# Attention of a two-layer kernel: heads taken in pairs, value matmuls of four heads together, all transposes in transpose mode

## What is computed

```python
qkv = einsum('bnc,fc->bnf', layernorm(x), w_qkv)     # 12 heads of 16 channels, 4 images, 256 tokens
att = softmax(q @ k.T * SCALE)                        # 256 x 256 per head and image
att = softmax(att * mask)                             # mask is 0.5 where row % 64 == column % 64, else 1
out = (att @ v) @ w_out.T + b_out
```

## Time and profile before

| | us |
|---|---|
| median of 3 runs | 545.7 |
| lowest and highest run | 543.4, 549.63 |
| span of the profiled execution, first to last instruction | 538.7 |
| TensorE busy in the span | 477.6 |
| VectorE busy | 235.1 |
| ScalarE busy | 162.4 |
| GpSimd busy | 152.3 |

### The profile page before, as it was taken

One profiled execution on the slowest core, in us unless ns is written; L12 is line 12 of the kernel. 1 busy time (PEld: TensorE's weight loads), 2 busy tenths in 40 slices (PEclk: granted clock), 3 DMA queues, 4 the chain that ended last, 5 costly groups with the idle time before them and its releaser, 6 DMA issues.

```text
span 538.7 us, 7851 instructions
## 1 busy us (share of the span) xinstructions
PE 477.6 (89%) x2343; PEld 322.5 (60%) x2344; DVE 235.1 (44%) x676; ACT 162.4 (30%) x418; POOL 152.3 (28%) x135
## 2 busy tenths in 40 slices
PE   0999999999998169899999999889999999999990
PEld 0554766565656147766676666655767666666660
DVE  5157232222222344676666665638623333333330
ACT  2142002111112023466656565442012111121210
POOL 2000115556655100000000000000125565566652
PEclk9999699999999669899999999999899999999996
DMA  9992111222220593000000003764211221221100
GB/s 265 209 350 67 35 52 23 39 38 35 39 27 9 141 331 135 1 1 0 2 1 1 1 2 83 181 174 112 77 38 31 33 25 26 34 35 23 12 0 0
DMA packets 20956, 36.20 MB, mean 67 GB/s; under 512 B 6544, under 2 KB 17481, under 8 KB 20484
## 3 DMA queue, kind: packets, MB, share of 16 engines
q1 hardware_dynamic: 10468, 29.56, 19.3%
q0 software_dynamic: 10464, 6.33, 8.4%
HBM read 31.92 MB, written 8.45 MB: 75 GB/s over the span
## 4 chain that ended last, share of the span: by engine, by line
PE 69%; DMA 15%; DVE 6%; issue 5%; ACT 1%; POOL 1%; POOLq 1%; SPq 0%; DVEq 0%
PE bank L1158 15%; DMA sum<-y,slot_tok 12%; PE bank L1333 9%; PE bank L1097 8%; PE bank L1173 6%; PE bank L1320 6%; PE bank L1127 4%; PE bank L1275 4%; PE bank L1289 3%; PE bank L1165 2%; PE bank L1322 2%; PE bank L1368 2%; PE bank L1134 1%; PE bank L1079 1%; PE bank L1304 1%
## 5 line engine op out<-in xcount | busy, mean ns | idle before, releaser
L473 POOL DMA_INDIRECT rows<-xn_rows,slot_tok x56 | 58.4, 1042 | 131.5 <-DVEq L800 90.6
L1158 PE MATMUL bank<-w_first,rows_t 96*128 x248 | 85.4, 487 | 0.2 <-issue 0.2
L1173 PE MATMUL bank<-w_second,hid_t 128*128 x370 | 71.4, 333 | 8.3 <-issue 6.3
L859 DVE TENSOR_SCALAR y<-bank,slot_w 128x192 f32<-128x192 f32 x54 | 22.6, 418 | 102.5 <-PE bank L1173 83.6
L1173 PEld LDWEIGHTS bank<-w_second,hid_t 128*128 128x128 f32 x370 | 58.7, 190 | 13.5 <-issue 13.1
L484 POOL DMA_INDIRECT out<-y,slot_tok x31 | 48.9, 1577 | 47.4 <-DMA out<-y,slot_tok 28.2
L1158 PEld LDWEIGHTS bank<-w_first,rows_t 96*128 96x128 f32 x248 | 44.6, 190 | 25.5 <-issue 0.7
L631 ACT ACTIVATE scratch<-bank,neg_max 128x256 f32<-128x256 f32 x96 | 44.6, 470 | 39.2 <-DVE neg_max L948 34.4
L1333 PE MATMUL bank<-scratch,w_first 128*32 128x256 f32 x192 | 50.9, 390 | 0.0
L522 POOL COPY act_h<-o_inv 128x256 f32<-128x256 f32 x12 | 4.8, 400 | 162.7 <-DVE o_inv L979 162.0
L484 POOL DMA_INDIRECT sum<-y,slot_tok x23 | 36.3, 1577 | 36.3 <-DMA sum<-y,slot_tok 23.7
(11 more groups left out here) (172 smaller groups left out, 649.3 us busy)
## 6 DMA issues: line engine op xcount, KB each, us to landing
w_first<-in_gate_up SPq DMA_DIRECT2D x16, 576.0 KB
w_second<-in_down SPq DMA_DIRECT2D x1, 4608.0 KB, 24.5
w_first<-in_fc SPq DMA_DIRECT2D x1, 3072.0 KB
w_second<-in_fc SPq DMA_DIRECT2D x1, 3072.0 KB, 28.5
xn_rows<-xn_tok SPq DMA_DIRECT2D x2, 768.0 KB, 5.9
rows<-xn_rows,slot_tok POOLq DMA_INDIRECT x56, 2.7
w_first<-in_x_t SPq DMA_DIRECT2D x2, 384.0 KB, 4.4
w_first<-in_w SPq DMA_DIRECT2D x1, 768.0 KB, 7.0
```

The source lines that it names most:

```text
L473: pool.indirect_dma_start(rows[b % 2][:], None, xn_rows[L.l], bass.IndirectOffsetOnAxis(slot_tok[:, b:b + 1].bitcast(U32), 0), bounds_chec ...
L1158: ins = pe.matmul(bank[:, 5 + g, 0:I1], rows_t[0:CH, k, :], w(CH, (k * 2 + g) * I1, I1), start=(k == 0), stop=(k == NCH - 1))
L1173: ins = pe.matmul(bank[:, 1, 0:C], hid_t[:, tile(ic)], w(P, ic * C, C), start=(ic == 0), stop=(ic == L.IC - 1))
```

## The change

Two heads now make one unit of work p (24 of them) in every step of the attention: one reduction over two banks, four exponentials, one reciprocal and four products (in place in `e1`), eight transposes to banks 4 and 5, one exponential over 1024 elements. All transposes are in transpose mode. The value matmuls of a chunk stand together once its second pair is ready, ordered by key tile and within it by head, so that neighbours write to different column groups. The sums stand in bank 6 beside the values and the spread inverses in bank 7. The buffers are regrouped: `p2_t` takes the room of `xn_t` and `g_sh` for two of its three. The steps of each engine are written in a new order. In the diff, lines that are only "..." mark what is left out.

```diff
-        e1 = [scratch_at(512 * i, 2, TOKENS_IMG) for i in range(3)]
-        att = [scratch_at(512 * (3 + i), 2, TOKENS_IMG) for i in range(2)]
-        p2_t = [scratch_at(512 * (5 + i), 2, TOKENS_IMG) for i in range(3)]
+        e1 = [scratch_at(1024 * i, 4, TOKENS_IMG) for i in range(3)]
+        p2_t = [scratch_at(3072, 4, TOKENS_IMG),
+                xn_t_room[:, 0, :].rearrange("p (a b) -> p a b", a=4),
+                g_room[:].rearrange("p a (b c) -> p (a b) c", b=2)]
...
         N_HEADS = IMAGES * HEADS
...
+        N_PAIRS = N_HEADS // 2
+        N_CHUNKS = N_HEADS // HPC
+        PAIRS_CHUNK = HPC // 2
+        def chunk_at(p, lag):
+            c = (p - lag + 1) // PAIRS_CHUNK - 1
+            if c == N_CHUNKS - 1 or (p - lag + 1) % PAIRS_CHUNK or c < 0 or c >= N_CHUNKS:
+                return None
+            return c
+        SUMS_AT = TOKENS_IMG
...
-            sp.wait_ge(sc_ps, N_HEADS)
+            sp.wait_ge(sc_ps, N_PAIRS)
...
...
+            def exp_scores(p):
+                act.wait_ge(nmax_ready, p + 1)
+                if p >= 3:
+                    act.wait_ge(att_t_ps, p - 2)
+                for q in range(4):
+                    ins = nc.scalar.activation(e1[p % 3][:, q, :], bank[:, 2 * (p % 2) + q // 2, (q % 2) * 256:(q % 2 + 1) * 256],
+                                               ACT.Exp, bias=neg_max[:, p % 4, q:q + 1],
+                                               accum_out=exp_sum[:, p % 4, q:q + 1])
+                ins.then_inc(e1_ready, 1)
+            def exp_att(p):
+                act.wait_ge(att_t_ps, p + 1)
+                if p >= 3:
+                    act.wait_ge(av_ps, (p - 3) // PAIRS_CHUNK + 1)
+                nc.scalar.activation(p2_t[p % 3].rearrange("p a b -> p (a b)"),
+                                     bank[:, 4:6, :].rearrange("p a b -> p (a b)"), ACT.Exp).then_inc(p2_ready, 1)
...
-            for n in range(N_HEADS + 3):
-                if n < N_HEADS:
-                    exp_scores(n)
-                if 0 <= n - 2 < N_HEADS:
-                    exp_att(n - 2)
-                if chunk_at(n, 3) is not None:
-                    out_copy(chunk_at(n, 3))
+            exp_scores(0)
+            exp_scores(1)
+            for p in range(N_PAIRS):
+                if p + 2 < N_PAIRS:
+                    exp_scores(p + 2)
+                exp_att(p)
+                if chunk_at(p, 1) is not None:
+                    out_copy(chunk_at(p, 1))
+            out_copy(N_CHUNKS - 1)
...
-            def neg_maximum(n):
-                dve.wait_ge(sc_ps, n + 1)
-                v.tensor_reduce(neg_max[:, n % 4, :], bank[:, n % 4, :].rearrange("p (a b) -> p a b", a=2),
+            def neg_maximum(p):
+                dve.wait_ge(sc_ps, p + 1)
+                b = 2 * (p % 2)
+                v.tensor_reduce(neg_max[:, p % 4, :], bank[:, b:b + 2, :].rearrange("p b (a k) -> p (b a) k", a=2),
                                 AXX, ALU.max, negate=True).then_inc(nmax_ready, 1)
...
-            def attention(n):
-                dve.wait_ge(e1_ready, 2 * n + 2)
-                if n >= 2:
-                    dve.wait_ge(att_t_ps, n - 1)
-                go(v.reciprocal(exp_inv[:, n % 2, :], exp_sum[:, n % 4, :]))
-                for qt in range(2):
-                    ins = v.scalar_tensor_tensor(att[n % 2][:, qt, :], e1[n % 3][:, qt, :], exp_inv[:, n % 2, qt:qt + 1],
+            def attention(p):
+                dve.wait_ge(e1_ready, p + 1)
+                go(v.reciprocal(exp_inv[:, p % 2, :], exp_sum[:, p % 4, :]))
+                for q in range(4):
+                    ins = v.scalar_tensor_tensor(e1[p % 3][:, q, :], e1[p % 3][:, q, :], exp_inv[:, p % 2, q:q + 1],
                                                  mask, ALU.mult, ALU.mult)
-                    if qt == 0:
+                    if q < 3:
                         step(ins)
                 ins.then_inc(att_ready, 1)
...
-            for n in range(ATT_STEPS):
-                if 2 <= n < N_HEADS:
-                    neg_maximum(n)
-                if 0 <= n - 1 < N_HEADS:
-                    attention(n - 1)
-                if n == N_HEADS:
-                    ln_stats(0)
-                if chunk_at(n, SUMS) is not None:
-                    invert_sums(chunk_at(n, SUMS))
-                if n == ATT_STEPS - 1:
-                    ln_rows(2, 0)
-                if chunk_at(n, SUMS + 2) is not None:
-                    out_norm(chunk_at(n, SUMS + 2))
-                if (chunk_at(n, SUMS + 3) or 0) % HC == HC - 1:
-                    residual(chunk_at(n, SUMS + 3) // HC)
+            for p in range(N_PAIRS):
+                if p + 2 < N_PAIRS:
+                    neg_maximum(p + 2)
+                attention(p)
+                if chunk_at(p, 2) is not None:
+                    invert_sums(chunk_at(p, 2))
+                if chunk_at(p, 3) is not None:
+                    out_norm(chunk_at(p, 3))
+                if (chunk_at(p, 4) or 0) % HC == HC - 1:
+                    residual(chunk_at(p, 4) // HC)
+            ln_stats(0)
+            out_norm(N_CHUNKS - 2)
+            invert_sums(N_CHUNKS - 1)
+            ln_rows(2, 0)
+            out_norm(N_CHUNKS - 1)
+            residual(IMAGES - 1)
...
-            def scores(n):
-                pair, img = (n, n + 1), n // HEADS
-                if n >= 4:
-                    pe.wait_ge(e1_ready, 2 * (n - 2))
+            def scores(p):
+                pair, img = (2 * p, 2 * p + 1), 2 * p // HEADS
+                if p >= 2:
+                    pe.wait_ge(e1_ready, p - 1)
                 for qt in range(2):
                     q0 = img * TOKENS_IMG + qt * P
                     for part in (k_high, k_low):
...
                             ins = pe.matmul(bank[:, m % 4, qt * 256:(qt + 1) * 256], q_parts[r, h // HPC, q0:q0 + P],
                                             part[r, h // HPC, img * TOKENS_IMG:(img + 1) * TOKENS_IMG],
                                             start=(part is k_high), stop=(part is k_low))
-                            if qt == 1 and part is k_low:
-                                ins.then_inc(sc_ps, 1)
+                ins.then_inc(sc_ps, 1)
             pe.wait_ge(parts_ready, 2 * QKC)
             scores(0)
+            scores(1)
...
-            def att_transpose(n):
-                pe.wait_ge(att_ready, n + 1)
-                if n >= 2:
-                    pe.wait_ge(p2_ready, n - 1)
+            def att_transpose(p):
+                pe.wait_ge(att_ready, p + 1)
+                if p:
+                    pe.wait_ge(p2_ready, p)
+                for m in range(2):
+                    for kt in range(2):
+                        for qt in range(2):
+                            ins = pe.transpose(bank[:, 4 + m, (kt * 2 + qt) * P:(kt * 2 + qt + 1) * P],
+                                               e1[p % 3][:, 2 * m + qt, tile(kt)], ident)
+                ins.then_inc(att_t_ps, 1)
+            def weigh_values(c):
+                pe.wait_ge(p2_ready, PAIRS_CHUNK * (c + 1))
+                if c:
+                    pe.wait_ge(o_raw_ready, c)
+                    pe.wait_ge(inv_ready, c)
+                img = c // HC
                 for kt in range(2):
-                    for qt in range(2):
-                        dst = bank[:, 4 + n % 2, (kt * 2 + qt) * P:(kt * 2 + qt + 1) * P]
-                        src = att[n % 2][:, qt, tile(kt)]
-                        if kt == qt:
-                            ins = pe.matmul(dst, src, ident, start=True, stop=True)
-                        else:
-                            ins = pe.transpose(dst, src, ident)
-                ins.then_inc(att_t_ps, 1)
-            def weigh_values(n):
-                img, h = n // HEADS, n % HEADS
-                g, c = n % HPC, n // HPC
-                pe.wait_ge(p2_ready, n + 1)
-                if g == 0 and c:
-                    pe.wait_ge(o_raw_ready, c)
-                for kt in range(2):
-                    ins = pe.matmul(bank[g * HG:(g + 1) * HG, 6, 0:TOKENS_IMG],
-                                    v_tok[:, 2 * img + kt, h, :], p2_t[n % 3][:, kt, :],
-                                    start=(kt == 0), stop=(kt == 1))
+                    for g in range(HPC):
+                        p = c * PAIRS_CHUNK + g // 2
+                        ins = pe.matmul(bank[g * HG:(g + 1) * HG, 6, 0:TOKENS_IMG],
+                                        v_tok[:, 2 * img + kt, (c % HC) * HPC + g, :], p2_t[p % 3][:, 2 * (g % 2) + kt, :],
+                                        start=(kt == 0), stop=(kt == 1))
                 ins.then_inc(av_ps, 1)
...
-            for n in range(ATT_STEPS):
-                if n % 2 and n + 1 < N_HEADS:
-                    scores(n + 1)
-                if 0 <= n - 2 < N_HEADS:
-                    att_transpose(n - 2)
-                if 0 <= n - 3 < N_HEADS:
-                    weigh_values(n - 3)
-                if chunk_at(n, SUMS) is not None:
```

(67 more changed lines are left out.)

22 lines of the change are left out of this document (5 added, 17 removed).

## The result

| | before | after |
|---|---|---|
| median of 4 runs, us | 547.66 | 611.61 |
| lowest, highest | 543.4, 552.43 | 608.3, 617.42 |
| span of the profiled execution | 538.7 | 612.1 |

The ratio is 1.1215, 95% interval 1.1119 to 1.131: 64 us slower. The changed kernel's profiled execution took 614.11, 2.0 us more than its span, and all executions in this study whose span is known took 1.8 to 2.2 us more. So the kernel before's profiled execution took near 541 and was faster than the median, and the 7.0 us that the prediction laid around the span were 5 too many. Executions of one kernel can lie 2% and more apart, the longer ones with a lower mean clock, and a profile shows one execution only, which in the kernels lag, lag_act, lag_act_oldT, lag_act_fill, before_values and before_values_newT was one of the longer ones.

The account below looks back on a forecast made before the run. It took TensorE, 89% busy, as the bound. Span 538.7 + 38 for the new order + 38 for the low clock = 615, with 7.0 around the span about 621, given as 620; range 581 to 652.

Parts of the forecast that it names:

- the ring: Attention in the new order: TensorE and VectorE each wait while the other works, 4.92 us a step.
- values fully overlapped: Rival for the value matmuls: four column groups at once, 1.0 us a chunk for 2.1; result 603, chance 0.17.
- Part 1: Attention transposes: 96 go from 0.22 to 0.11 us, 10 us less TensorE work, and 7 us less between transposes and values.
- Part 2: Value matmuls in four column groups: 2.1 us a chunk instead of 3.92, 22 us of TensorE work saved.
- nine slots of 16: Value matmuls: a second record runs only beside the next matmul's first, so nine slots of some 0.23 us, 2.1 us.
- Part 3: Attention order by pairs: last projection starts at 385.6 instead of 347.70, +38 us at full clock.
- Part 4: TensorE's clock in the attention: falls to 1.2 GHz in waits and returns at times, 38 us of at most 66.
- The clock that never returns: Rival for TensorE's clock in the attention: it stays low and the whole 66 us is paid; 650, chance 0.16.
- the sentence of the Trainium skill beside it: Transposes in transpose mode do not count as activity for the full clock; by it the whole 66 us would be paid.
- Full clock: Rival for TensorE's clock in the attention: it stays full; result 584, chance 0.09.
- No ring: Rival for the attention order: scores are ready before transposes hold TensorE up, VectorE ends last; about 512, chance 0.06.

Follow-up runs that it names:

- lag: The changed kernel with its transposes, and all engines' work on chunks, one step later; 539.96 us.
- lag_act: The kernel of lag with ScalarE's two jobs of a step exchanged, the exponentials of the transposes before those of the scores; 511.47 us.
- lag_act_oldT: The kernel of lag_act with two transposes a head put back to matmuls with the identity; 523.04 us.
- lag_act_fill: The kernel of lag_act with one more matmul per pair, 128x128 by 128x256 on constants, result overwritten; 515.54 us.
- before_values: The kernel before, in its own order and transposes, with only the value matmuls of a chunk taken together over four column groups, with seven p2_t buffers; 518.24 us.
- before_values_newT: The kernel of before_values with all transposes in transpose mode; median 536.54 us, three runs 535.55 to 537.94 and one 523.39.
- before_newT: The kernel before with all transposes in transpose mode and nothing else; 534.80 us.
- per_head: The changed kernel with a chunk's value matmuls ordered by head and within it by key tile; 610.62 us.
- filler2: The changed kernel with two added matmuls, 128x128 by 128x512 on constants, between scores and transposes of each step; 567.68 us.
- fillerT: The kernel of filler2 with its two added matmuls replaced by 16 transposes of 128x128 in transpose mode; 568.49 us.
- ring_oldT: The changed kernel with two transposes of each head put back to matmuls with the identity; 628.27 us.

## Why the prediction was right, and where its terms were off

The forecast was 620 in a range of 581 to 652, the result 611.61. The direction and its cause, the ring with a low clock in it, were right. That the number came so near is in part luck: the forecast's own account of the values was wrong and that of a rival, priced at 603, was right, and errors of the other sign in the clock brought the result back to halfway between the two.

- **Part 1** (10 us of TensorE's work for the transpose form): shown by before_newT, 10.4 us. The 7 us beside it, for fewer changes between transposes and values, no run shows by itself.
- **Part 2** (values at 2.1 us a chunk, nine slots of 16): mis-sized. The step that failed is that a matmul's second record must keep the next group waiting. The changed kernel takes 1.00 us, the lower end of what was given, and per_head shows that the program order within the chunk does not matter. Twelve times 1.1 us is 13 us too much at full clock. The Trainium skill (TensorE: Matmul & The Clock Gate, "Measured speedup vs the span model") has 2.38 times for three column tiles. The 1.65 us estimated from it was nearer, and still above: four took a quarter of the time.
- **Part 3** (the ring, 4.92 us): shown by lag, and term by term by the rows. Predicted 0.78, 3.06 and 1.08; measured 0.82, 3.07 and 1.03. The sum has 169.3 us from the first scores to the last projection (385.6 less 216.3). With values at 1.0 it is 156.1 at full clock; in filler2 and fillerT, at 0.95 and 0.96, it took 155.0 and 157.5.
- **Part 4** (the clock, 38 us of at most 66): right in kind, sized low. With the values' measured 1.86 us at the low clock the most is 53 us, to which the v matmuls (L1308) add: most of them ran at 0.50 where the earlier trace rows has 1.00, some 4 us. Measured were some 45 us of these 57 (200.6 less 155.0), four fifths and not six tenths. Why the clock fell already there is not settled, but it is not the changed order alone: filler2, ring_oldT, lag and per_head have the same order up to there and ran the v matmuls at 1.00, fillerT and lag_act for the most part at 0.50 as the changed kernel did.
- From the unrounded sum, 621.7, to the result are 10 us. The values were 13 us too high and the rest of the ring 1, the clock 7 too low: 7 us less for the stage. It started 1.6 us later, and 2.6 more came behind it. The time around the span was 5 too much, and the median lies 2.5 below the profiled execution.
- The rivals: values fully overlapped is what happened. The clock that never returns fell by its own test, since it returned now and then, and the sentence of the Trainium skill beside it fell with fillerT. Full clock fell with the row of 0.60. No ring fell with the waits. What I wrote for a kernel without the ring, 512, is near what lag_act gives, 511.47. Its stage was 101.2 us where that sum has 98, with VectorE as the bound as I had said, so this is not the total alone; but the 5 us too many around the span are in the 512 too.

What remains open is how the clock and the gaps hang together in numbers. The runs show only that with TensorE busy without a gap the clock stayed at 1.00, and that gaps before the transposes of 3.1 us (changed kernel) and of 0.9 us on average, at most 1.3 (before_values_newT), went with 0.59 and 0.74, while in filler2 gaps of 1.1 us on average, at most 1.2, went with 0.94.

## What to carry to other kernels

Before merging steps into larger units, follow one unit's data around the engines and note at each stop what is queued ahead of it: if the next unit's first job stands behind this unit's last one on both engines, their times add, however well each part got faster. Take work out of TensorE only together with what ends last beside it, and look at the granted clock of the stage afterwards, since saved work can come back as a lower clock. Compare single runs and the changed stage too, and not the medians alone: here the unchanged part of the program differed by up to 14 us. The cure here was to delay the transposes by one step and to exchange two jobs on ScalarE.

## What was not expected of the hardware

- Four column groups run at once even for float32 matmuls of two records: 16 records in 1.00 us against 3.92 when they come a head at a time, and 1.03 in the other program order.
- More work made a kernel faster: 1.7 us more a step took 44 us off (611.61 to 567.68). In the old order 0.22 us more a head took 20 us off by the medians (536.54 to 516.45), but only 3 to 8 against the one faster run, 523.39.
- Float32 transposes in transpose mode held the clock up as matmuls did: 0.96 and 0.95 in the same stretch.
